# GpSimd normalises a group's attention result without waiting for VectorE's additions of tiles 8 and 9

## The chip, the cores and the metric

One core of a Trainium2 chip. TensorE multiplies, VectorE, ScalarE and GpSimd work on elements, SyncE issues the DMAs used here. The metric is the device time of one execution in microseconds (us); it is compared by the median of several runs.

## The reference

The kernel computes a block of a multimodal network: a gated cross-attention of 4 sequences of 512 rows and 512 columns over a context of 1,601 rows each, then a mixture of experts. Only the attention matters here. It has 16 heads of 32 columns. A row attends to 1,344 text rows and, with a softmax of its own, to 257 image rows, and the two results are added:

```python
def attention(q, k, v):
    scale = 1.0 / jnp.sqrt(jnp.asarray(HD, q.dtype))
    scores = jnp.einsum('bqhd,bkhd->bhqk', q, k) * scale
    probs = jax.nn.softmax(scores, axis=-1)
    return jnp.einsum('bhqk,bkhd->bqhd', probs, v)
...
img_x = attention(q, k_img, v_img)
txt_x = attention(q, k, v)
out = (txt_x + img_x).reshape(B, L, DIM)
return linear(out, o_w, o_b)
```

## The kernel before

The program has three stages: projections of queries, keys and values, attention, and the experts. Each engine has its own instruction stream, written by hand, and the engines meet at counting semaphores. Attention takes 16 **groups** G (4 heads of one sequence each; NG = 16), and each group 13 key **tiles** kt of 128 keys. A group is a walk over the steps kt = 0 to 12.

In each step TensorE makes four score products (L1147, one per head j, into three rotating PSUM banks), ScalarE turns each into exponentials in a buffer P (L1306; there are four P buffers, so tile kt+4 overwrites tile kt), and TensorE multiplies the exponentials of an earlier tile with the values (L1081). Between them TensorE computes 64 "units" (L1127), score products of the **next** group whose maxima VectorE takes (L1437) for the softmax's shift.

The softmax's denominators need the sum of the exponentials over tiles. The sum of tiles 0 to 9 is built in one buffer, `sacc`, 128x2048:

- GpSimd adds tiles 0 and 1 (L1581, two pieces), then tiles 2 to 6 and three quarters of tile 7 (L1587, in step 8): the **chain**, whose last link is the 128x1536 one.
- VectorE adds the last quarter of tile 7 (L1443, which waits for the chain's link of tile 6) and tile 8 (L1460, 128x2048) in step 11, and tile 9 in step 12 in two pieces (L1460, 128x1024 each). Between L1443 and tile 8 stands the last reduction of the maxima (L633), between tile 9's pieces the lower part of the row of maxima (L650), which SyncE sends to `Qst` (L328) as an input of the next group's scores.
- TensorE multiplies `sacc` with ones (L1081, ps<-sacc,ones) in step 0 of the next group, behind the last products with the values, and behind it in its stream come the next group's scores.

The result of group G is divided by its denominators during group G+1. The denominators go through HBM (`Td`, `Rd`) and come back as reciprocals, broadcast to 128 partitions, in `rt2` (SyncE, L1065, step 7). In step 12 GpSimd's function `normalise` multiplies the image result `oi` (L1596) and the text result `ot` (L1597) with them, and adds (L1599). ScalarE and VectorE split the sum for the output projection in step 1 of the group after (L1337, L1468). GpSimd's next chain starts in step 2 of that group.

`normalise(G-1)` runs in group G for G = 1 to 15. The last group's own sums are VectorE's alone (L1453), and its result is divided by VectorE. `d_add` counts VectorE's additions, four to a group; the value 4 * G + 8 in `normalise(G)` is thus reached at the second half of tile 9 of group G+1. In groups 5, 9 and 15 the output projection of the sequence before is woven into steps 4, 6, 8 and 10, which makes them longer.

Of the kernel before, what the change touches and what calls it, by code (L numbers as in the profile page):

```python
# [38 lines left out]
def program(nc, ap, ctx):  # L39
    pe, dve, act, pool, sp = nc.tensor, nc.vector, nc.scalar, nc.gpsimd, nc.sync  # L40

    def sem(name):
        return ctx.enter_context(nc.semaphore(name))
# [69 lines left out]
    d_add = sem("d_add")  # L113
# [174 lines left out]
    def all_projected(engine):  # L288

        engine.wait_ge(p_mm, NMM)  # L290
        engine.wait_ge(d_mm, NMM)
        engine.wait_ge(p_tr, NTR)
        engine.wait_ge(a_tr, NTR)
        engine.wait_ge(d_tr, NTR)
        engine.wait_ge(g_cl, NCH)
        for i in range(2):
            engine.wait_ge(s_st[i], 32 * (NCH // 2))
            engine.wait_ge(s_v[i], 16 * ((NU + 1 - i) // 2))
# [686 lines left out]
    def exp_no(G, kt, j):  # L985
        return 52 * G + 4 * kt + j + 1
# [15 lines left out]
    def sum_no(G, kt):  # L1002
        return 8 * G + max(1, kt) + 1
# [11 lines left out]
    def slot(G, kt):  # L1015
        return (NKT * G + kt) % 4
# [554 lines left out]
    def pool_attend():  # L1571
        all_projected(pool)

        def first_sum(G):

            if G:
                pool.wait_ge(p_tot, 5 * (G - 1) + TEXT_TOTAL)
            for j in (0, 2):
                pool.wait_ge(a_exp, exp_no(G, 1, j + 1))
                h = slice(j, j + 2)  # L1580
                pool.tensor_tensor(sacc[:, h], P[slot(G, 0)][:, h], P[slot(G, 1)][:, h], ALU.add).then_inc(g_sum, 1)  # L1581

        def add(G, kt):
            pool.wait_ge(a_exp, exp_no(G, kt, 3))
            pool.wait_ge(g_sum, sum_no(G, kt) - 1)
            h = slice(0, 3 if kt == 7 else 4)
            pool.tensor_tensor(sacc[:, h], sacc[:, h], P[slot(G, kt)][:, h], ALU.add).then_inc(g_sum, 1)  # L1587


        def normalise(G):  # L1590
            ot = ot2[:, G % 2, :]
            pool.wait_ge(d_add, 4 * G + 8)
            pool.wait_ge(a_txt, 2 * G + 1)
            pool.wait_ge(a_img, 2 * G + 1)
            pool.wait_ge(s_den, 112 * (G + 1))
            pool.tensor_tensor(oi[:], oi[:], rt2[:, 1, :], ALU.mult).then_inc(g_oi, 1)  # L1596
            pool.tensor_tensor(ot, ot, rt2[:, 0, :], ALU.mult).then_inc(g_oi, 1)  # L1597
            pool.wait_ge(g_oi, 3 * G + 2)
            pool.tensor_tensor(ot, ot, oi[:], ALU.add).then_inc(g_oi, 1)  # L1599

        for step in range(NSTEP):
            G, kt = divmod(step, NKT)
            if G < NG - 1 and kt == 2:
                first_sum(G)
            if G < NG - 1 and 3 <= kt < 9:
                add(G, kt - 1)
            if step == 12:
                pool.wait_ge(a_woh, 4)
                pool.wait_ge(d_add, 4)
                for k in range(4):  # L1610
                    pool.tensor_tensor(Wol[:, k], wo[:, k], Woh[:, k].bitcast(F32), ALU.subtract).then_inc(g_wol, 1)
            if kt == 12 and 1 <= G < NG:
                normalise(G - 1)
# [728 lines left out]
```

## Time and profile before

| | us |
|---|---|
| median of 3 runs | 1707.87 |
| lowest and highest | 1707.13, 1708.17 |
| the profiled execution, its own time | 1711.98 |
| its span in the trace | 1710.4 |
| TensorE busy | 1668.2 (98%) |
| VectorE busy | 1184.7 (69%) |
| ScalarE busy | 831.6 (49%) |
| GpSimd busy | 900.4 (53%) |

The page's table of engines gives busy time over the span; a list of waits says who stood idle for whom; the timeline gives instructions in order of time. In a timeline a row may merge several instructions (x2, x6) and its duration is then from the first's start to the last's end. An instruction's duration also holds the time that it was begun but held up. PE is TensorE, PEld its weight load, DVE VectorE, ACT ScalarE, POOL GpSimd, SPq the queue of SyncE.

### The profile page before, as it was taken

How to read it: one execution, taken by the hardware profiler on the slowest of the kernel's cores; microseconds unless marked ns; L12 is line 12 of the kernel's file. 1: busy time of each engine (PE TensorE's matmuls, PEld its weight loads, DVE VectorE, ACT ScalarE, POOL GpSimd, SP SyncE). 2: the span in 40 equal slices, each digit the busy share in tenths (PEclk: the TensorE clock that was granted, in tenths of full speed). 3: DMA queues.
4: the chain of work that ended last, by engine and by line, in shares of the span. 5: the costliest groups of instructions: out<-in, count | busy, mean ns of one | idle time of the engine just before them, and what ended most of it. 6: DMA issues, size and time to landing. Idle time of an engine off the chain costs nothing. (4 is left out here: it accounts for less than half of the span.)

```text
span 1710.4 us, 24784 instructions
## 1 busy us (share of the span) xinstructions
PE 1668.2 (98%) x8694; PEld 1119.6 (65%) x8694; DVE 1184.7 (69%) x2220; ACT 831.6 (49%) x1550; POOL 900.4 (53%) x343
## 2 busy tenths in 40 slices
PE   6999999999999999999999999998999999999999
PEld 5888878886445555455554455445777778888777
DVE  6776677667888887888878888777444454443565
ACT  4443333326666664666556666662221355554221
POOL 3221311215777775788747777710605476775642
PEclk9999999999999999999999999999999999999999
DMA  9556858646556553565455555211314487886533
GB/s 332 167 158 195 242 173 210 195 151 195 154 153 159 147 149 66 154 159 159 137 139 145 157 136 141 101 39 42 136 38 155 163 267 258 271 270 198 174 103 99
DMA packets 198603, 277.34 MB, mean 162 GB/s; under 512 B 30968, under 2 KB 128008, under 8 KB 197964
## 3 DMA queue, kind: packets, MB, share of 16 engines
q1 hardware_dynamic: 192928, 258.91, 51.4%
q0 software_dynamic: 5120, 16.78, 2.9%
q8 instruction: 70, 1.15, 0.3%
q14 instruction: 53, 0.43, 0.1%
q10 hardware_dynamic: 432, 0.07, 0.0%
HBM read 202.21 MB, written 106.42 MB: 180 GB/s over the span
## 5 line engine op out<-in xcount | busy, mean ns | idle before, releaser
L1306 ACT ACTIVATE P<-ps 128x512 f32<-128x512 f32 (+1 forms) x832 | 444.8, 598 | 232.8 <-PE ps L1147 160.3
L1437 DVE TENSOR_REDUCE mp<-ps 128x1 f32<-128x448 f32 x720 | 411.8, 615 | 80.3 <-PE ps L1127 78.2
L1587 POOL TENSOR_TENSOR sacc<-sacc,P 128x2048 f32<-128x2048 f32 x90 | 397.7, 4419 | 16.4 <-ACT P L1306 5.5
L1127 PE MATMUL ps<-Kst,Qst 96*128 96x448 f32 x960 | 336.1, 371 | 2.7 <-DVE stl L626 1.7
L1147 PE MATMUL ps<-Qst,Kst 100*128 100x512 f32 (+1 forms) x832 | 323.5, 411 | 4.0 <-ACT P L1306 3.2
L1127 PEld LDWEIGHTS ps<-Kst,Qst 96*128 96x128 f32 x960 | 182.9, 191 | 156.7 <-DVE mp L1437 86.5
L1081 PE MATMUL ps<-P,Vg 128*32 128x512 f32 (+2 forms) x1664 | 217.5, 607 | 0.4 <-ACT P L1306 0.3
L822 POOL TENSOR_TENSOR cl<-craw,ch 128x1024 fp32r<-128x1024 f32 (+2 forms) x26 | 62.0, 2383 | 283.2 <-ACT ch L550 283.2
L1147 PEld LDWEIGHTS ps<-Qst,Kst 100*128 100x128 f32 (+1 forms) x832 | 153.1, 186 | 71.4 <-ACT P L1306 40.2
L49 PE MATMUL ps<-W,ch 128*128 128x512 f32 (+1 forms) x408 | 162.5, 398 | 0.0
L51 PE MATMUL ps<-W,cl 128*128 128x512 f32 (+1 forms) x408 | 159.7, 392 | 0.0
L50 PE MATMUL ps<-W,ch 128*128 128x512 f32 (+1 forms) x408 | 159.4, 391 | 0.0
L2239 POOL TENSOR_TENSOR gul<-gur,guh 128x2048 fp32r<-128x2048 f32 x15 | 69.6, 4643 | 104.5 <-ACT guh L1934 103.0
L1437 DVE TENSOR_REDUCE mx<-ps 128x1 f32<-128x258 f32 x240 | 99.3, 414 | 7.9 <-PE ps L1127 7.8
L1581 POOL TENSOR_TENSOR sacc<-P 128x1024 f32<-128x1024 f32 x30 | 71.1, 2389 | 62.5 <-ACT P L1306 36.9
L2239 POOL TENSOR_TENSOR Kst<-gur,Kst 128x2048 fp32r<-128x2048 f32 x15 | 69.2, 4616 | 65.3 <-ACT Kst L1934 45.3
L1596 POOL TENSOR_TENSOR oi<-oi,rt 128x512 f32<-128x512 f32 x15 | 19.8, 1321 | 144.8 <-DVE sacc L1460 116.3
L1081 PEld LDWEIGHTS ps<-P,Vg 128*32 128x32 f32 (+2 forms) x1664 | 34.6, 108 | 84.5 <-issue 46.6
L51 PEld LDWEIGHTS ps<-W,cl 128*128 128x128 f32 (+1 forms) x408 | 75.8, 186 | 17.8 <-issue 0.2
L49 PEld LDWEIGHTS ps<-W,ch 128*128 128x128 f32 (+1 forms) x408 | 76.0, 186 | 15.3
L50 PEld LDWEIGHTS ps<-W,ch 128*128 128x128 f32 (+1 forms) x408 | 76.1, 186 | 15.2
L570 ACT ACTIVATE junk<-kf 128x512 f32<-128x512 f32 (+1 forms) x51 | 32.2, 631 | 108.7 <-DVE kf L691 108.7
(249 smaller groups left out, 3145.1 us busy)
## 6 DMA issues: line engine op xcount, KB each, us to landing
gur<-in_w_gate_up SPq DMA_DIRECT2D x23, 1024.0 KB, 7.7
Kst<-KHd SPq DMA_DIRECT2D x56, 320.0 KB, 4.9
Vd<-vf SPq DMA_DIRECT2D x50, 256.0 KB, 2.1
craw<-in_ctxT SPq DMA_DIRECT2D x24, 512.0 KB, 4.4
KHd<-sth SPq DMA_DIRECT2D x24, 512.0 KB, 3.5
KLd<-stl SPq DMA_DIRECT2D x24, 512.0 KB, 4.9
dnr<-in_w_down SPq DMA_DIRECT2D x23, 512.0 KB
xg<-Xg SPq DMA_DIRECT2D x23, 512.0 KB, 7.9
```

Source lines behind the costliest of these rows:

```text
L49: pe.matmul(out, ah, bh, start=first, stop=False)
L50: pe.matmul(out, ah, bl, start=False, stop=False)
L51: return pe.matmul(out, al, bh, start=False, stop=last)
L822: pool.tensor_tensor(cl[:, n % 3, :, 0:c1 - c0], craw[:, n % 3, :, 0:c1 - c0], ch[:, n % 2, :, 0:c1 - c0].bitcast(F32), ALU.subtract).then ...
L1081: ins = pe.matmul(ps[32 * j:32 * j + 32, bank, :], w(j), pt[p0:p1_, j, :], start=first, stop=last, tile_position=(p0, 32 * j))
L1127: ins = pe.matmul(ps[:, bank, 0:c1 - c0], Qst[G % 3][0:96, j, 128 * qt:128 * qt + 128], Kst[s][0:96, j, c0:c1], start=True, stop=True)
L1147: pe.matmul(ps[:m, 2 + (e - 1) % 3, :], Kst[s][0:100, j, 128 * kt:128 * kt + m], Qst[G % 3][0:100, j, :], start=True, stop=True).then_inc( ...
L1306: act.activation(P[slot(G, kt)][:m, j, :], ps[:m, 2 + (e - 1) % 3, :], ACT.Exp, scale=SCALE).then_inc(a_exp, 1)
L1437: dve.reduce_max(out, ps[:, bank:bank + k, 0:cols] if k > 1 else ps[:, bank, 0:cols], AX.X).then_inc(d_ra, 1)
L1581: pool.tensor_tensor(sacc[:, h], P[slot(G, 0)][:, h], P[slot(G, 1)][:, h], ALU.add).then_inc(g_sum, 1)
L1587: pool.tensor_tensor(sacc[:, h], sacc[:, h], P[slot(G, kt)][:, h], ALU.add).then_inc(g_sum, 1)
L2239: pool.tensor_tensor(gul[q % 2], gur[raw_slot(q)][:], guh[q % 2].bitcast(F32), ALU.subtract).then_inc(g_gu, 1)
```

## The change

`normalise(G)` no longer waits for VectorE's four additions of group G+1. Its other waits stay: the text and image result are in `ot` and `oi` (`a_txt`, `a_img`), and the reciprocals have landed (`s_den`). It keeps its place in GpSimd's stream, right behind the chain's last link, and no instruction of any engine changes its order.

```diff
         def normalise(G):
             ot = ot2[:, G % 2, :]
-            pool.wait_ge(d_add, 4 * G + 8)
             pool.wait_ge(a_txt, 2 * G + 1)
             pool.wait_ge(a_img, 2 * G + 1)
             pool.wait_ge(s_den, 112 * (G + 1))
             pool.tensor_tensor(oi[:], oi[:], rt2[:, 1, :], ALU.mult).then_inc(g_oi, 1)
             pool.tensor_tensor(ot, ot, rt2[:, 0, :], ALU.mult).then_inc(g_oi, 1)
             pool.wait_ge(g_oi, 3 * G + 2)
             pool.tensor_tensor(ot, ot, oi[:], ALU.add).then_inc(g_oi, 1)
```

## Rows read from the trace of the kernel before

**Rows 1.** Busy time in one whole group, us 744.60 to 790.06.

```profile
core 0: us, PE busy (x) PEld busy (x) DVE busy (x) ACT busy (x) POOL busy (x), PEclk, DMA share, GB/s
744.60:790.06 45.46, 45.33 (x273) 23.01 (x273) 38.96 (x73) 30.50 (x58) 35.04 (x12) 1.00 0.57 150
```

**Rows 2.** TensorE's waits, us 470 to 1140: waiting, for whom, total, times, longest.

```profile
PE ps L1147 <- ACT P L1306: 2.0, 8, 0.5
PE ps L49 <- DVE mp L1437: 0.3, 2, 0.2
PE ps L1081 <- ACT P L1306: 0.3, 1, 0.3
PE ps L1147 <- DMA Qst<-ms: 0.3, 1, 0.3
```

**Rows 3.** Waits of all engines in the same stretch.

```profile
POOL oi L1596 <- DVE sacc L1460: 116.3, 14, 19.1
...
POOL oi L1596 <- DMA rt<-Rd: 28.5, 1, 28.5
```

**Rows 4.** GpSimd's timeline in a regular group: start, duration, instruction, idle before.

```profile
762.58 3.48 POOL L1587 TENSOR_TENSOR sacc<-sacc,P 128x1536 f32<-128x1536 f32 x1
...
772.58 1.27 POOL L1596 TENSOR_TENSOR oi<-oi,rt 128x512 f32<-128x512 f32 x1 [6.52 <-DVE sacc L1460]
773.81 1.28 POOL L1597 TENSOR_TENSOR ot<-ot,rt 128x512 f32<-128x512 f32 x1
775.18 1.29 POOL L1599 TENSOR_TENSOR ot<-ot,oi 128x512 f32<-128x512 f32 x1
779.19 4.74 POOL L1581 TENSOR_TENSOR sacc<-P 128x1024 f32<-128x1024 f32 x2 [2.72 <-ACT P L1306]
```

**Rows 5.** VectorE's timeline in the same group.

```profile
761.68 1.14 DVE L1437 TENSOR_REDUCE mp<-ps 128x1 f32<-128x448 f32 x2
...
765.73 0.88 DVE L1443 TENSOR_TENSOR sacc<-sacc,P 128x512 f32<-128x512 f32 x1
766.54 0.19 DVE L633 TENSOR_REDUCE mx<-mp 128x16 f32<-128x48 f32 x1
766.75 2.29 DVE L1460 TENSOR_TENSOR sacc<-sacc,P 128x2048 f32<-128x2048 f32 x1
769.14 1.23 DVE L1460 TENSOR_TENSOR sacc<-sacc,P 128x1024 f32<-128x1024 f32 x1
770.69 0.68 DVE L650 TENSOR_TENSOR ms<-ps,ms 8x512 fp32r<-8x512 f32 x1 [0.33 <-ACT ms L646]
771.30 1.20 DVE L1460 TENSOR_TENSOR sacc<-sacc,P 128x1024 f32<-128x1024 f32 x1
772.43 1.14 DVE L1437 TENSOR_REDUCE mp<-ps 128x1 f32<-128x448 f32 x2
```

**Rows 6.** TensorE, ScalarE and SyncE around it, same group.

```profile
769.12 1.08 ACT L1306 ACTIVATE P<-ps 65x512 f32<-65x512 f32 x2 [0.42 <-issue]
...
770.68 2.05 PE L1081 MATMUL ps<-P,Vg 128*32 128x512 f32 x16
...
771.43 0.64 SPq L328 DMA_DIRECT2D Qst<-ms  x1
...
772.55 0.16 PEld L1081 LDWEIGHTS ps<-sacc,ones 128*32 128x32 f32 x8 [0.73 <-DVE sacc L1460]
772.56 1.06 PE L1081 MATMUL ps<-sacc,ones 128*32 128x512 f32 x8
...
773.76 0.60 ACT L1317 ACTIVATE ms<-ps 128x512 f32<-128x512 f32 x1 [2.15 <-DMA Qst<-ms]
...
773.92 0.47 PE L1147 MATMUL ps<-Qst,Kst 100*128 100x512 f32 x1
```

**Rows 7.** GpSimd and VectorE together, last group, from the timeline.

```profile
1135.50 1.23 DVE L1513 TENSOR_TENSOR Kst<-Vg,Kst 128x1024 fp32r<-128x1024 f32 x1
1135.92 1.96 POOL L1596 TENSOR_TENSOR oi<-oi,rt 128x512 f32<-128x512 f32 x1 [28.48 <-DMA rt<-Rd]
1136.64 3.38 DVE L1453 TENSOR_TENSOR sacc<-sacc,P 128x2048 f32<-128x2048 f32 x1
1137.84 3.33 POOL L1597 TENSOR_TENSOR ot<-ot,rt 128x512 f32<-128x512 f32 x1
```

**Rows 8.** GpSimd's back-to-back L815 and VectorE's L727, projection stage, from the timeline.

```profile
31.73 1.48 POOL L815 TENSOR_TENSOR W<-wraw,W 128x512 fp32r<-128x512 f32 x1
32.59 1.17 DVE L727 SCALAR_TENSOR_TENSOR xq<-xq,stq,bias 128x512 f32<-128x512 f32 x1
33.17 1.74 POOL L815 TENSOR_TENSOR W<-wraw,W 128x512 fp32r<-128x512 f32 x1
```

**Rows 9.** Group 5, from the timeline: end of chain, VectorE's L1443, normalise.

```profile
654.05 8.22 POOL L1587 TENSOR_TENSOR sacc<-sacc,P 128x2048 f32<-128x2048 f32 x2
...
674.69 0.68 DVE L1443 TENSOR_TENSOR sacc<-sacc,P 128x512 f32<-128x512 f32 x1
...
681.35 1.28 POOL L1596 TENSOR_TENSOR oi<-oi,rt 128x512 f32<-128x512 f32 x1 [19.07 <-DVE sacc L1460]
```

## The prediction

> **What bounds the kernel now.** I read the page's table of engines first: TensorE is busy 98% of the span. A share over the whole span says little about one place, so the next view is a single group of the attention stage. There TensorE is busy 45.33 of 45.46 us [rows 1], at a granted clock of 1.00. The list of TensorE's waits over nearly all of attention confirms it: 2.9 us in all, of which none is for GpSimd [rows 2]. So a group's length is TensorE's own work, and whatever is freed elsewhere has at most those 2.9 us to give.
>
> The largest wait in the same list is GpSimd's, in front of `normalise`: 116.3 us, 14 times, for VectorE's additions [rows 3]. It is this wait that the change removes. One more, before the fifteenth `normalise`, is for the DMA of the reciprocals (28.5 us) and stays. GpSimd's timeline shows that nobody pays for the 116.3 us: `normalise` ends at 776.47, and the next chain starts at 779.19, after another 2.72 us of waiting for ScalarE [rows 4]. ScalarE and VectorE take the result up only after that and have no wait for it.
>
> **What the change removes.** In a regular group the chain's last link ends at 762.58 + 3.48 = 766.06, and `normalise` starts at 772.58 [rows 4]. Now it starts at 766.06. What was removed was no path to the end, so the gain is nothing, with 2.9 us over the whole stage as its upper bound.
>
> **What the change adds** is company. From 766.06 on VectorE does its additions to `sacc`, and these are of the one kind that collides. The trace shows such a meeting in the last group [rows 7]. L1513 (both inputs in SBUF) runs until 1136.73. GpSimd's L1596 is begun at 1135.92 but takes 1.96 us instead of 1.27, and ends at 1137.88, 1.15 us behind L1513's end. VectorE's L1453, begun at 1136.64, takes 3.38 us where it takes 2.29 alone as L1460 does [rows 5]: it ends at 1140.02, 2.14 behind GpSimd's end. L1597 ends at 1141.17, 1.15 behind that. So only one of the two engines works at a time, a held one finishes in its own duration less about 0.13 us (its start-up is done while it is held), and the two alternate. The regular group shows the same already: L1443 is begun at 765.73, while the chain's last link runs, and ends at 766.61, 0.55 behind it, with 0.88 us instead of the 0.68 of group 5 [rows 5, 9].
>
> What decides the sum is who goes first when GpSimd has its next instruction ready and VectorE is held. Such a moment is in the projection stage [rows 8]. GpSimd's L815 ends at 33.21, another L815 is right behind it, and L727 of VectorE has been held since 32.59. L727 ends at 33.76, 0.55 behind the first L815, and the second takes 1.74 us to 34.91, 1.15 behind L727. So the held engine gets in between. Reductions of PSUM (L1437), L633 and L650 have at most one input in SBUF. Two of L1437 take 1.14 us at 761.68, beside GpSimd's chain, and 1.14 us at 772.43 [rows 5], so I count these as free.
>
> The Trainium skill bears on this (SBUF — State Buffer, § Who interferes with whom): a VectorE instruction with two SBUF inputs and a GpSimd instruction that reads SBUF block each other for the whole of an instruction, by order of issue. It speaks against the change, and rows 7 and 8 agree with it.
>
> **The sum for one regular group**, by these rules (held: 1.15 for a 128x512 of GpSimd, 2.14 for VectorE's 128x2048, and for its 128x1024 1.23 - 0.15 = 1.08 and 1.20 - 0.15 = 1.05) [rows 4, 5, 7]:
>
> - L1443 ends at 766.61, as before, and L633 at 766.73.
> - L1596 ends at 766.61 + 1.15 = 767.76.
> - Tile 8, ready at 766.75, ends at 767.76 + 2.14 = 769.90, before at 769.04.
> - L1597 ends at 771.05.
> - Tile 9's first half ends at 771.05 + 1.08 = 772.13, before at 770.37.
> - L1599 has to wait for L1597's semaphore until about 771.15, and is held until 772.13: it ends at 773.28.
> - L650 follows the first half and ends at about 772.75, before 771.37.
> - Tile 9's second half, ready at 772.7, ends at 773.28 + 1.05 = 774.33. Before it ended at 771.30 + 1.20 = 772.50.
>
> So `sacc` is complete 1.83 us later. Who waits: TensorE's product of `sacc` with ones. It started at 772.56, its weight load being released by that very addition, while the product before it ends at 770.68 + 2.05 = 772.73 [rows 6]. The cover is at most 0.17 us, and since the matmuls are shown to overlap at their edges I take it as 0. Queued behind this product on TensorE are all scores of the new group. TensorE's other inputs are late too, but less. Tile 8's delay of 0.86 us holds the exponentials of tile 12 (ScalarE at 769.12, 0.08 behind tile 8's end), and with them the last product with the values. That is within the 1.83. The row of maxima leaves SyncE at 772.8 instead of 771.43. It took until 773.76, 2.33 us, to land [rows 6], so now it lands at 775.1, while TensorE wants it only at 773.92 + 1.83 = 775.75. Once TensorE is late, everything that it feeds is late with it, GpSimd's next chain too, which starts on exponentials of step 1. So the next group meets the same pattern, and since TensorE has no idle time the loss isn't won back.
>
> **How many groups.** The 116.3 us in 14 waits have 19.1 as their longest [rows 3], that of group 5 [rows 9]. Group 9 has the same shape, and (116.3 - 2 x 19.1) / 12 = 6.5, the regular group's 6.52 [rows 4], in each of the other 12. In group 5 the chain ends at 662.27, and VectorE comes to L1443 only at 674.69 [rows 9], so in groups 5 and 9 `normalise` (3.9 us) is over long before. In group 15 the DMA decides as before. 12 x 1.83 = 22.0 us. Nothing else in the program changes. The profiled execution would have a span of 1710.4 + 22.0 = 1732.4 and a time of 1711.98 + 22.0 = 1734.0. It ran 4.1 us above the median of the runs, so for the median I say 1707.87 + 22.0 = **1729.8**, 1.3% slower.
>
> **The rivals.**
>
> *The handover is dearer.* If a held instruction needs its full duration behind the other's end (1.27, 2.29, 1.28, 1.23, 1.29, 1.20), the list above ends at 766.61 + 8.56 = 775.17, 2.67 us late: 12 x 2.67 = 32.0, 1739.9. If GpSimd instead keeps its turn at 766.06, L1443 ends 1.24 later, and the list ends at about 775.1: 12 x 2.6 = 31, 1739. Rows 7 and 8 speak against both. The same skill page (§ A bandwidth-pool intuition that's wrong) reports a blocked operation starting some 115 ns behind the holder's end. By that figure, an estimate, six handovers add 0.7 us to the 2.67, and the time would be about 1748. No row here shows such a gap.
>
> *Part of it is hidden.* ScalarE or TensorE has some slack that the ends of matmuls, which are modelled, don't show, or `normalise` slips through one VectorE piece cheaper, since L1599 and L650 could coincide. With 0.5 to 1.0 us a group this gives 1714 to 1720.
>
> *Not slower.* Additions on VectorE and `normalise` run side by side, or are held for less than TensorE's cover. The place is the product of `sacc` at 772.56, and the point from which it decides is 0.17 us: with `sacc` late by less than that, TensorE never notices. Then the time is 1707.9, or down to 1705 if some of the 2.9 us of waits goes. For it speaks that GpSimd's three instructions are small (3.9 us in a group of 45.46). Against it speak rows 7, where a VectorE addition lost 1.1 us beside one of them. To this case I add that the change does nothing because the reciprocals aren't there yet at 766.06. Their DMAs are issued in step 7, four steps ahead, so I give that little.
>
> **How the numbers follow.** Forecast (1.1 to 2.3 us a group, 1721 to 1735.5): 0.66. Dearer handover (to 1748): 0.12. Partly hidden (1712 to 1720): 0.12. Not slower: 0.10, of it 0.03 for a gain that shows. The range takes the forecast's own bounds and the near part of both neighbours: 1719 to 1740. A measurement can tell about 0.2% from no change, 3.4 us: faster 0.03, same 0.07, slower 0.90.
>
> **What the profile will show.** GpSimd's idle time before L1596 goes from 6.5 us to nothing in 12 groups. L1596, L1597 and L1599 last about 1.8, 3.3 and 2.1 us instead of 1.3. Tile 8 takes 3.15 us instead of 2.29 and L1443 stays at 0.88. The list of TensorE's waits gains about 1.8 us a group, before the product of `sacc` and before tile 12's product with the values, and a regular group lasts 47.3 us instead of 45.5, while groups 5 and 9 keep their length. I'm wrong if VectorE's additions keep their durations (no collision), if L1443 lasts 2.1 us (GpSimd kept its turn), or if the additions are late and the group is not longer (cover that I didn't see).

## The result

The changed kernel takes 1727.83 us (median of 4 runs, 1727.67 to 1728.94), the kernel before 1708.02 (1707.13 to 1708.87): a ratio of 1.0116, with a 95% interval of 1.0102 to 1.013, or 19.8 us more. It is slower, as forecast, by a little less than the 22.0 us of the sum. On another chip, beside the last experiments, the same kernel took 1732.38 us against 1710.74, 1.012 (1.0092 to 1.0148), 21.6 us more.

The page of the kernel after has VectorE and GpSimd busier, though neither has an instruction more. These are its lines of span and engines (busy time, share of the span, instructions):

```profile
span 1727.4 us, 24769 instructions
...
PE 1671.1 (97%) x8694; PEld 1117.8 (65%) x8694; DVE 1212.0 (70%) x2220; ACT 832.1 (48%) x1550; POOL 940.9 (54%) x343
```

VectorE went from 1184.7 to 1212.0 us, GpSimd from 900.4 to 940.9: 27.3 and 40.5 us more, in which an instruction was begun and held. GpSimd's timeline in the group of [rows 4] (the lines of `normalise` are one number lower now, L1595, L1596 and L1598):

```profile
771.47 3.48 POOL L1587 TENSOR_TENSOR sacc<-sacc,P 128x1536 f32<-128x1536 f32 x1
774.91 1.74 POOL L1595 TENSOR_TENSOR oi<-oi,rt 128x512 f32<-128x512 f32 x1
776.62 3.32 POOL L1596 TENSOR_TENSOR ot<-ot,rt 128x512 f32<-128x512 f32 x1
780.02 2.14 POOL L1598 TENSOR_TENSOR ot<-ot,oi 128x512 f32<-128x512 f32 x1
```

The idle time of 6.52 us is gone, and the three instructions take 7.2 us instead of 3.8. VectorE's timeline beside it, to be held against [rows 5]:

```profile
774.63 0.88 DVE L1443 TENSOR_TENSOR sacc<-sacc,P 128x512 f32<-128x512 f32 x1
...
775.64 3.17 DVE L1460 TENSOR_TENSOR sacc<-sacc,P 128x2048 f32<-128x2048 f32 x1
778.91 2.11 DVE L1460 TENSOR_TENSOR sacc<-sacc,P 128x1024 f32<-128x1024 f32 x1
780.95 0.67 DVE L650 TENSOR_TENSOR ms<-ps,ms 8x512 fp32r<-8x512 f32 x1
781.55 1.69 DVE L1460 TENSOR_TENSOR sacc<-sacc,P 128x1024 f32<-128x1024 f32 x1
```

The two engines alternate. L1443 ends at 775.51, L1595 at 776.65, tile 8 at 778.81, L1596 at 779.94, tile 9's first half at 781.02, L1598 at 782.16, the second half at 783.24. From L1443's start to the end of the last addition it is 8.61 us, and it was 6.77 [rows 5]: `sacc` is complete 1.84 us later. TensorE waits for it. Its timeline at this place:

```profile
780.33 2.18 PE L1081 MATMUL ps<-P,Vg 128*32 128x512 f32 x16
783.30 1.07 PE L1081 MATMUL ps<-sacc,ones 128*32 128x512 f32 x8 [0.79 <-DVE sacc L1460]
```

and its waits from group 1 into group 14 (us 449 to 1106), which were 1.3 us in all in the same stretch before:

```profile
PE ps L1081 <- DVE sacc L1460: 8.7, 11, 0.8
PE ps L1147 <- ACT P L1306: 6.1, 13, 0.5
PE ps L49 <- DVE mp L1437: 0.3, 2, 0.2
```

The second line is tile 8's lateness: ScalarE may not overwrite its buffer, and TensorE waits for tile 12's exponentials. One whole group, from one L1595 to the next, in the table of busy times (for [rows 1]):

```profile
core 0: us, PE busy (x) PEld busy (x) DVE busy (x) ACT busy (x) POOL busy (x), PEclk, DMA share, GB/s
774.91:822.17 47.26, 45.78 (x276) 23.00 (x272) 41.19 (x73) 30.45 (x58) 38.36 (x13) 1.00 0.55 144
```

TensorE's busy time is 45.33 before and 45.78 now (waits inside merged matmuls count as busy), and the group is 47.26 us instead of 45.46.

**Where the 20 us are.** The starts of GpSimd's chains mark the groups. From the chain of group 1 to that of group 14 it was 616.64 us (448.06 to 1064.70), and is 636.59 (448.23 to 1084.82): 19.95 us more over 11 groups with the collision, 1.81 each. Groups 5 and 9 lie in between and kept their length (58.03 us each, 58.05 and 57.99 before). From there to GpSimd's first instruction of the experts (1200.17, now 1221.18) it is 0.9 us more. Together with 0.2 us ahead of group 1 that makes 21.0. The profiled spans differ by less, 1710.4 and 1727.4. Of these 4 us, 3 were lost by the profiled execution of before in its experts: the granted clock was 0.98 from 1200 to 1300, and the stretch up to the next L2239 that writes `gul` took 94.5 us against 91.5 after. The last 1 us isn't traced.

### The profile page after: what moved, and what is told of

It is laid out like the page before. It is cut to its first block and busy times, and to the rows that moved or that the text cites. A ratio compares the mean times of both kernels' runs of the same rounds, so it can differ in the third digit from the quotient of the medians.

```text
span 1727.4 us, 24769 instructions
## 1 busy us (share of the span) xinstructions
PE 1671.1 (97%) x8694; PEld 1117.8 (65%) x8694; DVE 1212.0 (70%) x2220; ACT 832.1 (48%) x1550; POOL 940.9 (54%) x343
## 3 DMA queue, kind: packets, MB, share of 16 engines
q8 instruction: 70, 1.15, 0.3%
## 5 line engine op out<-in xcount | busy, mean ns | idle before, releaser
L1460 DVE TENSOR_TENSOR sacc<-sacc,P 128x1024 f32<-128x1024 f32 (+1 forms) x45 | 97.8, 2173 | 1.9
```

The lines of the kernel that those rows point to most:

```text
L1460: dve.tensor_tensor(sacc[:, h], sacc[:, h], P[slot(G, kt)][:, h], ALU.add).then_inc(d_add, 1)
```

## The experiments

The theory: VectorE's additions and GpSimd's instructions that read SBUF exclude each other, `sacc` is complete later, and TensorE, which has no time to spare, waits. Rivals are that the early result or the removed wait costs by itself, that any company of GpSimd costs, and that the loss comes by another way than `sacc`. In each diff `normalise` is the function of the change. The kernel before had a median of 1707.3 to 1707.4 beside eight of them, 1711.2 beside the one with two reductions, and 1710.7 beside the last two.

**GpSimd writes and doesn't read.**

```diff
-            pool.tensor_tensor(oi[:], oi[:], rt2[:, 1, :], ALU.mult).then_inc(g_oi, 1)
-            pool.tensor_tensor(ot, ot, rt2[:, 0, :], ALU.mult).then_inc(g_oi, 1)
+            pool.memset(oi[:], 0.25).then_inc(g_oi, 1)
+            pool.memset(ot, 0.25).then_inc(g_oi, 1)
...
-            pool.tensor_tensor(ot, ot, oi[:], ALU.add).then_inc(g_oi, 1)
+            pool.memset(ot, 0.5).then_inc(g_oi, 1)
```

> The kernel after, but normalise's three GpSimd instructions only write oi and ot (128x512 each, a constant); the division by the denominators and the sum of text and image are left out. They start as early as after the change. Theory (VectorE's additions are held while GpSimd reads SBUF): the writes hold nobody, every addition keeps its length (tile 8 at 2.29 us), a regular group lasts 45.5 us, 1708. Rival A (any GpSimd instruction beside VectorE's additions holds them, writes too): 1712 to 1730, by the length of the writes. Rival B (it is the early result, the changed order of buffers and signals, that costs): 1728 as after the change.

Measured: 1706.92 us, ratio 1.0002 (0.9992 to 1.0012). Group 1 to group 14 took 616.65 us, before 616.64. From its timeline:

```profile
766.06 0.53 POOL L1595 MEMSET oi<- 128x512 f32 x1
766.52 0.53 POOL L1596 MEMSET ot<- 128x512 f32 x1
...
765.80 0.89 DVE L1443 TENSOR_TENSOR sacc<-sacc,P 128x512 f32<-128x512 f32 x1
...
766.82 3.62 DVE L1460 TENSOR_TENSOR sacc<-sacc,P 128x2048 f32<-128x2048 f32 x2
```

The writes lie beside L1443 and tile 8 and hold nobody: 3.62 us for tile 8 and the first half, as before. So neither the missing wait nor the early signals cost anything, and, since `normalise` is as early here as it can be, an early result gains nothing either. Both rivals A and B are out.

**A dose: one or two instructions early.**

```diff
-            pool.wait_ge(d_add, 4 * G + 8)
...
             pool.tensor_tensor(oi[:], oi[:], rt2[:, 1, :], ALU.mult).then_inc(g_oi, 1)
+            pool.wait_ge(d_add, 4 * G + 8)
             pool.tensor_tensor(ot, ot, rt2[:, 0, :], ALU.mult).then_inc(g_oi, 1)
```

> The wait for VectorE's additions is back, but between normalise's first product (oi) and its second. Computes all. Theory: only the first product meets an addition. Tile 8 ends 0.86 us late, and sacc is complete 0.85 us late, in 12 groups: 10.2 us, 1718. Rival (the cost is all or nothing, with the wait itself): 1708 or 1728.

In the next kernel the wait stands one line lower:

> The wait for VectorE's additions is back between normalise's second product and its sum. Theory: two instructions meet additions. The list of the prediction then ends at 773.90 instead of 772.50, 1.40 us late in 12 groups: 16.8 us, 1725. Rival (all or nothing): 1708 or 1728.

Measured: 1717.16 us (1.0065, 1.0048 to 1.0081) and 1724.53 us (1.0096, 1.0079 to 1.0113). The additions of one group in the first and in the second (VectorE's timeline):

```profile
769.12 0.88 DVE L1443 TENSOR_TENSOR sacc<-sacc,P 128x512 f32<-128x512 f32 x1
...
770.13 4.49 DVE L1460 TENSOR_TENSOR sacc<-sacc,P 128x2048 f32<-128x2048 f32 x2
...
775.55 1.20 DVE L1460 TENSOR_TENSOR sacc<-sacc,P 128x1024 f32<-128x1024 f32 x1
```

```profile
772.20 0.88 DVE L1443 TENSOR_TENSOR sacc<-sacc,P 128x512 f32<-128x512 f32 x1
...
773.22 5.38 DVE L1460 TENSOR_TENSOR sacc<-sacc,P 128x2048 f32<-128x2048 f32 x2
...
779.12 1.20 DVE L1460 TENSOR_TENSOR sacc<-sacc,P 128x1024 f32<-128x1024 f32 x1
```

The last addition ends 7.63 and 8.12 us behind L1443's start, 0.86 and 1.35 more than before; expected were 0.85 and 1.40. Groups got longer by 0.87 and 1.33 (9.55 and 14.6 us over 11). The whole change has 1.84 and 1.81. The cost is a sum of held instructions.

TensorE meets this lateness at another place in the first of the two. Its waits there (us 449 to 1106) hold none for `sacc`, and this line, which is 0.4 us in 2 waits before the change:

```profile
PE ps L1147 <- ACT P L1306: 6.0, 13, 0.5
```

Tile 8 and `sacc` are late by the same 0.86 us there. Tile 12's exponentials, which wait for tile 8, come first in TensorE's stream and take up the whole delay, part of it inside merged matmuls.

**TensorE's cover, without GpSimd.** The kernel before, with one, two or three (k) extra reductions on VectorE. They read one tensor in SBUF, and GpSimd stands idle beside them, so they collide with nothing:

```diff
+                for i in range(k):
+                    dve.reduce_max(fill[:, i:i + 1], P[slot(G, 9)][:, 2, :], AX.X)
                 add_to_sum(G, 9, slice(2, 4))
```

> The kernel before, with one more reduction on VectorE (128x512 of P, a single input in SBUF) ahead of the second half of tile 9. Nothing of GpSimd changes. This measures TensorE's cover by itself. Theory (cover 0 to 0.17 us): sacc is complete 0.55 to 0.65 us late in 15 groups (0 to 14), of which 0.4 to 0.65 shows: 6 to 10 us, 1714 to 1718. Rival (TensorE has slack there, and the loss after the change comes by tile 8 and ScalarE): under 3 us.

> The kernel before with two more reductions on VectorE ahead of the second half of tile 9, nothing of GpSimd changed. TensorE's idle time before the product of sacc should be 1.0 to 1.1 us in one piece (0.4 with one reduction, 1.6 with three, where the granted clock fell in some groups). Theory: sacc 1.2 us late, a group 1.15 longer, 14 groups: 16 us more than before, and the clock stays at 1.00 in the regular groups. Rival (the clock falls already): over 19 us more.

> The kernel before, with three more reductions (128x512 of P, one input in SBUF) on VectorE ahead of the second half of tile 9, nothing of GpSimd changed. One such reduction made sacc 0.60 us late and a group 0.555 us longer. Theory (the cover is 0.05 us and the rest shows in full): sacc about 1.7 to 1.8 us late, a group 1.7 longer over 14 or 15 groups, 1730 to 1733. So the lateness of the change's size costs as much without any collision. Rival (tile 8's lateness and ScalarE carry part of the change's cost): under 1.3 us a group, below 1727.

Measured, with the length of a regular group from the chains' starts:

| reductions | `sacc` late by | group longer by | TensorE idle before the product | median (before) | ratio (interval) |
|---|---|---|---|---|---|
| 1 | 0.60 | 0.555 | 0.4 | 1713.5 (1707.4) | 1.004 (1.0026 to 1.0054) |
| 2 | 1.18 | 1.15 | 1.0 | 1732.74 (1711.2) | 1.0106 (1.0076 to 1.0135) |
| 3 | 1.78 | 1.74, in groups at full clock | 1.6 | 1753.05 (1707.3) | 1.0283 (1.0215 to 1.0351) |

The cover is 0.03 to 0.05 us, and the rest of a lateness shows in full; with three reductions the sum is nearly as late as after the change (1.78 against 1.84) and a group pays nearly the same, 1.74 against 1.81, with no collision at all. So a late `sacc` alone is enough for the whole loss, and tile 8's lateness adds nothing to it: TensorE only meets a part of the same delay earlier.

The totals of the second and third row were not as expected; their medians are 21.5 and 45.8 us above those of the kernel before. In the second, from group 1 to group 14, the granted clock stayed at 1.00 and the groups paid 15.0 us as expected. The rest came in group 15, where its clock was 0.87 in the profiled run, against 0.96 before (us 1111 to 1157), and behind it. The interval of its ratio is 13 to 23 us. It leaves room for both the expectation (16) and its rival (over 19), so only the trace tells what the clock did. The third row is told below.

**Groups 5 and 9 alone.**

```diff
-            pool.wait_ge(d_add, 4 * G + 8)
+            if G not in (4, 8):
+                pool.wait_ge(d_add, 4 * G + 8)
```

> The wait is taken away in groups 5 and 9 alone, the ones with output projections, where the chain ends 12 us before VectorE's first addition. Theory: normalise starts 19 us earlier there and meets only reductions: no cost and no gain, within 2 us of 1708. Rival (each removal costs, or an early result helps): 2 x 1.8 us more, or less than before.

Measured: 1706.98 us, ratio 0.9994 (0.9983 to 1.0005). Neither cost nor gain. GpSimd's timeline in group 5, where each instruction has its length alone:

```profile
662.36 1.30 POOL L1597 TENSOR_TENSOR oi<-oi,rt 128x512 f32<-128x512 f32 x1
663.62 1.29 POOL L1598 TENSOR_TENSOR ot<-ot,rt 128x512 f32<-128x512 f32 x1
664.99 1.28 POOL L1600 TENSOR_TENSOR ot<-ot,oi 128x512 f32<-128x512 f32 x1
```

**One input instead of two.**

```diff
-            pool.tensor_tensor(oi[:], oi[:], rt2[:, 1, :], ALU.mult).then_inc(g_oi, 1)
+            pool.tensor_scalar(oi[:], oi[:], 0.001, None, ALU.mult).then_inc(g_oi, 1)
```

and likewise for the other two.

> The kernel after, with normalise's three instructions replaced by ones that read a single input (a tensor times a constant, 128x512); the division by the denominators and the sum of text and image are left out. Theory (a GpSimd instruction that reads SBUF holds VectorE's additions, and is held, for its length): they are shorter alone, 0.5 to 0.8 us, but begun beside an addition they last until it is over, 1.5 us or more; the additions are held 0.3 to 0.6 us each, and c. 0.15 to 0.6 us a group remains: 1709 to 1716. Rival (only GpSimd instructions with two inputs collide): every one keeps its length alone, 1708.

Measured: 1709.19 us, ratio 1.001 (0.9998 to 1.0022), which by itself can't be told from no change. The timeline (both engines) shows more:

```profile
766.92 0.89 DVE L1443 TENSOR_TENSOR sacc<-sacc,P 128x512 f32<-128x512 f32 x1
767.21 1.94 POOL L1595 TENSOR_SCALAR oi<-oi 128x512 f32<-128x512 f32 x1
...
767.93 2.48 DVE L1460 TENSOR_TENSOR sacc<-sacc,P 128x2048 f32<-128x2048 f32 x1
...
769.12 2.64 POOL L1596 TENSOR_SCALAR ot<-ot 128x512 f32<-128x512 f32 x1
```

Tile 8 takes 2.48 us instead of 2.29, and a regular group 45.7 instead of 45.5 (618.82 us for 616.64, from group 1 to group 14, 0.2 for each of the 11). A reader of one tensor holds the additions too, for less long. It isn't the instruction of 0.5 to 0.8 us that was expected. In group 5 of this run, with no addition beside it, it takes longer than the product of two tensors (1.30):

```profile
663.50 1.49 POOL L1595 TENSOR_SCALAR oi<-oi 128x512 f32<-128x512 f32 x1
```

**Who goes first.**

```diff
-            pool.wait_ge(d_add, 4 * G + 8)
+            pool.wait_ge(d_add, 4 * G + 6)
```

> normalise waits for VectorE's addition of tile 8, not for tile 9's two halves (the value waited for is 2 smaller). GpSimd's first product and tile 9's first half are released by the same signal; who comes first decides. If GpSimd: tile 9's first half ends 1.1 us late, the sum is complete 1.1 to 1.2 us late in 14 groups: 1722 to 1724. If VectorE: the first half keeps its length, the first product lasts 2.3 us and lies beside L650, the second half is held under 0.2 us: 1708 to 1710. Rival (no matter who starts, both share): both lengthen by a part, 1714.

Measured: 1722.05 us, ratio 1.0081 (1.0061 to 1.01). GpSimd was first, in all 14 groups. The lines are from both engines' timelines:

```profile
775.94 1.28 POOL L1596 TENSOR_TENSOR oi<-oi,rt 128x512 f32<-128x512 f32 x1 [3.06 <-DVE sacc L1460]
775.96 2.33 DVE L1460 TENSOR_TENSOR sacc<-sacc,P 128x1024 f32<-128x1024 f32 x1
```

Begun 0.02 us earlier, the product keeps its 1.28 us, and the addition takes 2.33 instead of 1.23. The loss of this meeting is all on the one that came second.

**An extra reduction after the change.** The kernel after with the one reduction of above, and the kernel after again beside it:

> The kernel after, with one more reduction on VectorE ahead of the second half of tile 9. The reduction runs while that half would be held by GpSimd's sum anyway (from 781.55 to 782.16 in the regular group after the change), so most of it is hidden: sacc gets 0.0 to 0.15 us later than after the change in the 12 colliding groups, 0.55 in groups 0, 5 and 9: 1729 to 1732. Rival (a held addition isn't only waiting, and the reduction adds its full 0.6 us): 1735 to 1737.

> The kernel after, again, beside the two others on one chip: 1727 to 1729.

Measured: 1734.3 us (1.0127, 1.01 to 1.0154) and 1732.38 us (1.012, 1.0092 to 1.0148), where the kernel before took 1710.74. The absolute times lie 4 us above what was expected, those of the kernel before 3 us; the difference of the two is 1.9 us, which the intervals don't separate from nothing. Before the change the same reduction cost 6. The traces are clearer: a regular group is 0.08 us longer (47.40 for 47.32, the mean of 11), groups 5 and 9, where nothing is held, 0.62 and 0.52 (58.63 for 58.01, 58.56 for 58.04). A held addition would only wait, and most of the work put in front of it is hidden.

## Why the prediction was right

**What bounds the kernel.** Right: TensorE without slack, so no gain. The write-only kernel shows it at 1.0002.

**The collision and its order.** Right in each line. The ends were forecast, from L1443's end on, as +1.15, +3.29, +4.44, +5.52, +6.67 and +7.72 us; measured are +1.14, +3.30, +4.43, +5.51, +6.65 and +7.73. `sacc` was forecast 1.83 us late and is 1.84. Both lengths and the alternation came from two short stretches of the trace of before [rows 7, 8], with other operations and in other stages. That a held instruction ends 0.13 us sooner than its length alone is shown; the reason given for it, a start-up done while it is held, is argued.

**The cover.** Taken as 0, measured as 0.03 to 0.05 us.

**Number of groups.** 12 were counted in full. Eleven cost 1.81 each; from the twelfth, group 14, to the experts only 0.9 us came on top. This is the mis-sized term of the sum. In group 15 there are no units to put between the product of `sacc` and its first scores, and TensorE before the change stood waiting for the row of maxima, which the change delays less than `sacc`:

```profile
1103.54 1.06 PE L1081 MATMUL ps<-sacc,ones 128*32 128x512 f32 x8
...
1104.90 0.93 PE L1147 MATMUL ps<-Qst,Kst 100*128 100x512 f32 x3 [0.29 <-DMA Qst<-ms]
```

After the change, at the same place:

```profile
1125.51 1.07 PE L1081 MATMUL ps<-sacc,ones 128*32 128x512 f32 x8 [0.79 <-DVE sacc L1460]
1126.50 0.97 PE L1147 MATMUL ps<-Qst,Kst 100*128 100x512 f32 x3
```

The product is 21.97 us later, the scores 21.60. That is 0.37 of the 0.9 us that are missing there. Most of the rest lies in a low clock of group 15, which both kernels have. The rows are of the table of busy times with the columns of [rows 1], the granted clock third from the end, first before and then after the change:

```profile
1112.00:1114.00 2.00, 1.52 (x4) 0.56 (x3) 1.95 (x1) 2.00 (x6) 0.00 (x0) 1.00 0.03 8
1114.00:1116.00 2.00, 2.00 (x10) 0.59 (x13) 1.84 (x2) 1.45 (x3) 0.00 (x0) 0.56 0.06 8
1116.00:1118.00 2.00, 2.00 (x13) 0.26 (x5) 0.79 (x1) 0.00 (x0) 0.00 (x0) 0.58 0.00 0
```

```profile
1134.00:1136.00 2.00, 1.51 (x4) 0.76 (x3) 1.98 (x1) 2.00 (x5) 0.00 (x0) 0.72 0.03 8
1136.00:1138.00 2.00, 2.00 (x9) 0.40 (x12) 1.87 (x1) 1.18 (x3) 0.00 (x0) 0.50 0.05 8
1138.00:1140.00 2.00, 2.00 (x15) 0.68 (x7) 0.43 (x1) 0.30 (x1) 0.00 (x0) 0.93 0.00 0
```

After the change the fall comes earlier in the same work, and the 16 products with the values that it slows take 2.84 us (from 1136.39) instead of 3.42 (from 1114.59). Behind them TensorE is 21.22 us late (1117.94, now 1139.16), 0.38 less than at the first scores. The last 0.2 us isn't separated. The row of the wait for the DMA, 0.3 us, stood in [rows 2], and the prediction passed over it.

**The remainder.** 21.0 us is the loss by the traces at the start of the experts, 19.8 and 21.6 that of the medians on two chips, with intervals of 17.4 to 22.2 and 15.7 to 25.3. Between 21.0 and 22.0 the runs can't tell by time alone; the traces can.

**The rivals.** The dearer handover (2.67 us a group) didn't come: no length is above the forecast. GpSimd didn't keep its turn either, since L1443 has its 0.88 us. Nothing was hidden in the regular groups. The 115 ns between the holder's end and the blocked operation stand in the Trainium skill (SBUF — State Buffer, § A bandwidth-pool intuition that's wrong) for a DMA whose descriptors GpSimd can't write while VectorE copies. They don't carry over to this pair: a held product ends 1.14 us behind the holder, 0.13 sooner than its length alone. The Trainium skill's rule of exclusion (SBUF — State Buffer, § Who interferes with whom) holds wherever a GpSimd instruction with two inputs met an addition, and so does its exemption of a GpSimd instruction that only writes, with the 3.62 us beside the writes. For one input the lock over the whole instruction doesn't fit the recorded ends, as is told below.

## What to carry to other kernels

A wait that an engine off the critical path sits in may be what keeps its memory traffic out of another's way: before removing it, list what the freed instructions will run beside, and whether both sides read SBUF with two inputs on VectorE and at least one on GpSimd. With two inputs on both sides the price was that of a strict alternation, and could be summed, from the lengths alone less 0.13 to 0.15 us for each held one, to a few hundredths of a microsecond; with one input on GpSimd it was 0.2 us a group and not 1.8. And ask who is released first; in each meeting the one that comes second pays.

## What the runs showed that was not expected

**TensorE's clock at a gap of 1.6 us.** With three extra reductions the kernel lost 46 us, where at most 26 were expected. TensorE's timeline in two groups of that run:

```profile
594.15 1.49 PE L1081 MATMUL ps<-sacc,ones 128*32 128x512 f32 x8 [1.60 <-DVE sacc L1460]
...
596.54 0.58 PE L1127 MATMUL ps<-Kst,Qst 96*128 96x448 f32 x1
```

```profile
800.13 1.06 PE L1081 MATMUL ps<-sacc,ones 128*32 128x512 f32 x8 [1.61 <-DVE sacc L1460]
...
801.67 0.37 PE L1127 MATMUL ps<-Kst,Qst 96*128 96x448 f32 x1
```

The same gap, but behind the first the granted clock is 0.66 and then 0.50 of full, the lower of the two levels, 1.2 GHz (table of busy times, three stretches of 2 us; the columns are those of [rows 1]):

```profile
594.00:596.00 2.00, 1.85 (x9) 0.58 (x10) 1.16 (x3) 0.30 (x1) 1.82 (x2) 0.66 0.52 104
596.00:598.00 2.00, 2.00 (x6) 1.70 (x6) 1.29 (x3) 1.32 (x3) 1.92 (x2) 0.50 0.67 190
598.00:600.00 2.00, 2.00 (x12) 1.34 (x15) 2.00 (x4) 1.26 (x3) 0.03 (x1) 0.98 1.04 218
```

Ahead of it TensorE had been idle 1.6 us in an otherwise full stretch, and such a group took 48.6 us, one without the fall 47.2. Of the 13 groups from 1 to 13 the clock fell below 1.00 in 8; the first two were longer still, 50.6 and 51.9 us at 0.91 and 0.89. With gaps of 0.4 and 1.0 us the regular groups all stayed at 1.00. So they did after the change, which loses as much time a group as three reductions, but in three pieces apart from each other (0.5, 0.5 and 0.8 us). What decides whether a gap of 1.6 us lowers the clock these runs don't show.

**A fall of the clock that some kernels miss.** The low clock of group 15, told above, doesn't come in every kernel. The stretch from 46 to 54 us behind the start of chain 14 ran at 0.79 before and after the change. With one reduction and with `normalise` behind tile 8 it ran at 1.00. From the start of chain 14 to the experts it was 135.5 us before, 134.1 and 134.4 in these two, though their `sacc` was late there too. So their totals hold a gain of over 1 us that the additions don't explain: one reduction costs 7.2 us from group 1 to group 14 and 6.1 by the medians. What decides whether the clock falls there isn't shown.

**A spread of 4 us in one kernel.** The kernel with two instructions early ran at 1722.5, 1722.6, 1726.5 and 1727.1. Its profiled run, the 1727.1, had a clock of 0.87 in group 15; in that of the change the stretch has 0.96, as before. Differences of 3 to 5 us between single runs or between two profiled spans are thus no sign of a kernel's own change; the starts of the chains are, from group 1 to group 14, where every run but the one with three reductions had a clock of 1.00.

**A GpSimd instruction with one input seems to let go early.** In the run with one input L1595 is recorded until 769.15, 1.34 us behind L1443's end, which is 0.15 less than its length alone, as with two inputs. But tile 8 ends at 770.41, only 1.26 us later. An addition of this size that was held by two inputs ended 2.14 to 2.16 us behind the holder's recorded end. If it needs as long here, it was released at about 768.27 (an estimate), 0.9 us before L1595's recorded end. Whether it was released then, or both shared the time, the runs don't separate.
